# First small loads on ScalarE's queue, new hand-written lists for the beginning and the end, and the FFN middle of the last two tiles in three column parts

## The reference: what is computed

```
states = scan(state @ A.T + x_t @ B.T)              # 16 states
out = layernorm(states @ C.T + x @ D.T) * gamma + beta
x = layernorm(x + out)
gate, up = fp4(x) @ fp4(w_gate).T, fp4(x) @ fp4(w_up).T    # 704 columns each
x = layernorm(x + fp4(silu(gate) * up) @ fp4(w_down).T)
```

## Time and profile before

| | |
|---|---|
| median of 3 runs | 566.85 us (566.63 to 566.96) |
| profiled execution, its own time | 566.68 us |
| its span (first to last instruction) | 564.9 us, so 1.8 us lie around it |
| busy share of the span | PE 98%, DVE 92%, ACT 83%, POOL 88% |
| granted clock of TensorE, mean | 0.998 |
| chain that ended last, by engine | PE 90%, DVE 5%, ACT 2% |

### The profile page before, as it was taken

How to read it: one execution, slowest core, us unless ns; L and a number is a source line. 1 busy time by engine, 2 the same in 40 slices (tenths; PEclk the granted TensorE clock), 3 DMA queues, 4 the chain that set the end, 5 groups by cost and what they waited for, 6 DMA issues and landing times.

```text
span 564.9 us, 12830 instructions
## 1 busy us (share of the span) xinstructions
PE 551.6 (98%) x3751; PEld 495.0 (88%) x3751; DVE 518.0 (92%) x1241; ACT 468.3 (83%) x1415; POOL 494.4 (88%) x674
## 2 busy tenths in 40 slices
PE   9899999999999999999999999999999999999995
PEld 7577779999999999999999999999999999999894
DVE  4896799999999999999999999999999999999973
ACT  3557867889888998988889898888989888898756
POOL 2566887999999999999999999999999999998653
PEclk9999999999999999999999999999999999999999
DMA  8951000011121111111211111121111122100001
GB/s 291 383 182 30 5 24 24 22 41 47 56 61 60 52 60 58 49 50 59 59 52 56 58 50 50 59 59 55 54 59 49 50 59 59 56 22 19 20 20 46
DMA packets 35772, 36.25 MB, mean 64 GB/s; under 512 B 6752, under 2 KB 34464, under 8 KB 34720
## 3 DMA queue, kind: packets, MB, share of 16 engines
q1 hardware_dynamic: 35744, 35.90, 20.1%
HBM read 19.50 MB, written 8.39 MB: 49 GB/s over the span
## 4 chain that ended last, share of the span: by engine, by line
PE 90%; DVE 5%; ACT 2%; issue 1%; POOL 0%; POOLq 0%; DVEq 0%; ACTq 0%
PE gu L1434 41%; PE turned L1434 18%; PE yb L1434 8%; PE turned L1517 7%; PE turned L1460 2%; PE yb L1448 1%; PE grid L1293 1%; PE turned L1541 1%; PE turned L1540 1%; PE gu L1345 1%; PE yb L1345 1%; DVE scratch L1095 1%; DVE scratch L1133 1%; PE gu L1381 1%; PE turned L1381 1%
## 5 line engine op out<-in xcount | busy, mean ns | idle before, releaser
L1434 PE MATMUL gu<-wguHi,xtHi 128*128 128x512 f32 (+1 forms) x384 | 151.3, 394 | 0.4 <-DVE xtLo L1088 0.4
L1434 PE MATMUL gu<-wguLo,xtHi 128*128 128x512 f32 (+1 forms) x384 | 143.7, 374 | 0.0
L1434 PE MATMUL gu<-wguHi,xtLo 128*128 128x512 f32 (+1 forms) x384 | 143.7, 374 | 0.0
L560 POOL TENSOR_TENSOR scratch<-scratch 128x704 f32<-128x704 f32 x63 | 90.7, 1439 | 3.2 <-DVE scratch L1109 2.6
L571 POOL TENSOR_TENSOR scratch<-scratch 128x640 f32<-128x640 f32 x64 | 81.4, 1271 | 7.6 <-DVE scratch L1133 7.4
L1434 PE MATMUL turned<-wdHi,htHi 128*128 128x256 f32 x295 | 83.7, 284 | 0.0
L1434 PE MATMUL turned<-wdHi,htLo 128*128 128x256 f32 x295 | 83.6, 283 | 0.0
L1434 PEld LDWEIGHTS gu<-wguHi,xtLo 128*128 128x128 f32 x384 | 72.2, 188 | 12.3
L1434 PE MATMUL turned<-wdLo,htHi 128*128 128x256 f32 x295 | 82.6, 280 | 0.0
L1434 PEld LDWEIGHTS gu<-wguHi,xtHi 128*128 128x128 f32 x384 | 72.2, 188 | 9.9 <-DVE xtLo L1088 1.1
L1434 PEld LDWEIGHTS gu<-wguLo,xtHi 128*128 128x128 f32 x384 | 72.4, 189 | 8.2
(11 more groups left out here) (225 smaller groups left out, 1679.7 us busy)
## 6 DMA issues: line engine op xcount, KB each, us to landing
xT<-in_L_attn_x_dram SPq DMA_DIRECT2D x8, 1024.0 KB, 9.9
scratch<-in_L_attn_x_dram SPq DMA_DIRECT2D x64, 128.0 KB, 2.4
out_dram<-scratch SPq DMA_DIRECT2D x64, 128.0 KB, 1.9
xtTile<-xT SPq DMA_DIRECT2D x48, 128.0 KB, 2.1
stTile<-statesHi SPq DMA_DIRECT2D x128, 8.0 KB, 1.7
stTile<-statesLo SPq DMA_DIRECT2D x64, 8.0 KB, 1.7
scratch<-in_L_ffn_w_down_dram SPq DMA_DIRECT2D x1, 704.0 KB, 10.3
scratch<-in_L_ffn_w_up_dram SPq DMA_DIRECT2D x1, 640.0 KB, 8.9
```

What stands on the lines that cost most here:

```text
L560: nc.gpsimd.tensor_tensor(blocks(hx[:, m % 2, :]), blocks(hx[:, m % 2, :]), each_block(hRc[:, m % 4, :], FB), ALU.mult).then_inc(s_xnh, 1)
L1434: ins = nc.tensor.matmul(to, l, r, start=(first and q == 0), stop=(last and q == len(passes) - 1))
```

## The change

Four things are changed. (1) The loads of D, C, A and B are issued by ACT and no longer by SP, and SP issues the last two weight loads ahead of the `tMat` copies. (2) All lists of the beginning are in another order, with 8 instead of 12 `unread` first, and `d_prep` and `w_recip` have their independent steps interleaved. (3) The last two tiles (`SPLIT = 2`) run their FFN middle in three parts of 256, 256 and 192 columns, products of gate and up included. (4) The end is written out as lists, without the `unread` of `is_ending` (one is left ahead of each of the last two `down`), and the last two tiles are normalised by one DVE operation (`norm_last`) instead of `nr3` and `norm3`.

```diff
-    VECTOR_COPIES = (0, 2, 7, 9, 14, 15, 17, 19, 23, 25, 28)
+    VECTOR_COPIES = (2, 3, 5, 9, 12, 15, 16, 17, 18, 19, 27, 28)
...
-            for i in range(last):
+            for i in range(last if eng is nc.sync else 0):
                 step(HALVES, i, False)
...
-        SPLIT = 1
+        SPLIT = 2
+        FIRST_SPLIT = TILES - SPLIT
+        PARTS = ((0, 2 * P), (2 * P, 4 * P), (4 * P, FF))
...
@@ SP @@
-                sp.dma_start(dRaw[:, :, :], D.rearrange("(k p) d -> p k d", p=P)).then_inc(s_dc, 16)
-                sp.dma_start(cRaw[:, :, :], C.rearrange("(k p) n -> p k n", p=P)).then_inc(s_dc, 16)
-                sp.dma_start(aRaw[:, :], A).then_inc(s_small, 16)
-                sp.dma_start(bRaw[:, :], B).then_inc(s_small, 16)
             load_x(0)
...
+            sp.dma_start(wg[:, full + 1:WG_ROWS, :],
+                         w_up[P - part:FF, :].rearrange("(r p) k -> p r k", p=P)).then_inc(s_wload[2], 16)
+            sp.dma_start(wX[:, WG_ROWS * H:].rearrange("p (r k) -> p r k", k=FF),
+                         w_down.rearrange("(r p) k -> p r k", p=P)).then_inc(s_wload[3], 16)
             sp.wait_ge(s_tDiag, 1)
             sp.wait_ge(s_pwc, POWER_COPIES[LOG_C + 1])
...
@@ ACT @@
+                nc.scalar.dma_start(dRaw[:, :, :], D.rearrange("(k p) d -> p k d", p=P)).then_inc(s_dc, 16)
+                nc.scalar.dma_start(cRaw[:, :, :], C.rearrange("(k p) n -> p k n", p=P)).then_inc(s_dc, 16)
+                nc.scalar.dma_start(aRaw[:, :], A).then_inc(s_small, 16)
+                nc.scalar.dma_start(bRaw[:, :], B).then_inc(s_small, 16)
...
@@ DVE @@
+            def norm_last(h, m):
+                r = m % RING
+                dve.wait_ge(s_st[r], done_dma(h, m - RING))
+                dve.wait_ge(s_pow3, done(h, m))
+                nc.vector.tensor_scalar(outTile[:, r, :], x1[:, m, :], nm3t[:, m:m + 1], rs3[:, m:m + 1], ALU.add,
+                                        ALU.mult).then_inc(s_out, 1)
...
@@ PE @@
-                if is_ending(h, m):
-                    unread(4, to)
...
+            def down_part(h, m, k):
+                tile, to = h * CHUNK + m, down_bank(h, m)
+                if k == 0:
+                    pe.wait_ge(s_x1p, TILES)
+                    pe.wait_ge(s_r, tile)
+                    unread(1, to)
+                pe.wait_ge(s_lo, part(tile, k))
...
-            unread(12, wbanks[1], ones)
+            unread(8, wbanks[1], ones)
```

More of the change, by code:

```diff
@@ new lines, in _ @@
+            ve3(7, 0)
+            nr3(6, 7)
+            ve1(7, 7)
+            norm3(6, 7)
+            norm2(7, 6)
+            silu_gate(7, 3)
+            nm3(7, 1)
+            nr3(7, 0)
+            sq3(7, 1)
+            norm3(7, 0)
+            h_hi(7, 2)
+            nm2(7, 7)
+            h_abs(7, 3)
+            silu_gate(7, 4)
+            sq2(7, 7)
+            x_abs(7, 6)
+            ve2(7, 7)
+            x_hi(7, 5)
+            ve3(7, 1)
+            nr2(7, 7)
+            norm2(7, 7)
@@ new lines, in _ @@
+            nr3(7, 1)
+            norm3(7, 1)
+            nm3(7, 2)
+            sq3(7, 2)
+            ve3(7, 2)
+            h_hi(7, 3)
+            h_abs(7, 4)
+            silu_gate(7, 5)
+            x_abs(7, 7)
+            nr3(7, 2)
+            norm3(7, 2)
+            x_hi(7, 6)
+            nm3(7, 3)
+            sq3(7, 3)
+            silu_part(7, 6, 0)
+            ve3(7, 3)
+            h_hi(7, 4)
+            h_abs(7, 5)
+            silu_part(7, 6, 1)
+            nr3(7, 3)
+            norm3(7, 3)
@@ L1542, in ffn_down, with up_part, columns @@
                                  stop=True).then_inc(s_dn, 1)
+            def up_part(h, m, k):
+                tile, (a, b) = h * CHUNK + m, PARTS[k]
+                if k == 0:
+                    pe.wait_ge(s_xlo, done(h, m))
+                if is_split(tile - 1):
+                    pe.wait_ge(s_h, part(tile - 1, k))
+                else:
+                    pe.wait_ge([s_silu, s_h, s_hsc][k], tile)
+                def columns(w, c):
+                    return w[:, c, :].rearrange("p (g f) -> p g f", g=2)[:, :, a:b]
+                split_products(gu_part(k), [((xtHi[:, m % 2, c, :], xtLo[:, m % 2, c, :]),
+                                             (columns(wguHi, c), columns(wguLo, c))) for c in range(KH)]).then_inc(s_gate, 1)
@@ new lines, in turn_part @@
+            def turn_part(h, m, k):
+                tile = h * CHUNK + m
+                if k == 2:
+                    pe.wait_ge(s_lo, part(tile, 0))
+                elif is_split(tile - 1):
+                    pe.wait_ge(s_lo, part(tile - 1, 2 if k == 0 else 1))
+                else:
+                    pe.wait_ge(s_lo, tile)
+                pe.wait_ge(s_xlo, TILES)
+                pe.wait_ge(s_qh, part(tile, k))
+                for q in range(2):
+                    row = KD[2 * k + q]
+                    rows = hq[:, m % 2, row:row + P] if row + P <= FF else hTail[:, m % 2, :]
+                    ins = nc.tensor.transpose(ht_parts[k][:, q * P:(q + 1) * P], rows, ident[:, :])
+                ins.then_inc(s_t, 1)
```

748 lines of the change are left out of this document (482 added, 266 removed).

## The result

The changed kernel takes **584.82 us** (median of 5, 584.21 to 585.64) where the kernel before took 566.85 beside it: a ratio of 1.0316, interval 1.0296 to 1.0335. That is 18 us slower, where 1.5 us faster was forecast, and far outside the range. Both halves of the sum were wrong, the beginning most.

What follows compares the result with a forecast made beforehand. TensorE, busy 98% of the span, was taken to bound the kernel, its steady part unchanged. Beginning +2.9 and end −3.9 − 0.5 = −4.4 gave −1.5 us, 565.3 against the median of 566.85; range 560.8 to 568.2.

Steps and rivals of the forecast that it cites:

- The small loads now share the engines with x, so I let them land where they did.: Beginning, ACT's queue: D, C, A and B land when they did before, while x goes out 2.0 us sooner.
- Fillers, −1.8: Start of the kernel: eight filler matmuls instead of twelve unread's worth make TensorE ready 1.8 us earlier.
- I keep 2.4 GHz in the sum.: TensorE's clock, both halves: stays at full rate although fillers go, since the end's waits are short and split by products.
- Rival 2: Wait ahead of link(0, 8): the clock falls there, half rate loses another 2.7 us, whole +1.9, 568.7 us; chance 0.20.
- the third rival: End: DVE's extra operations bind the last two tiles, half of the gain is left, about 567.5 us; chance 0.10.
- The new wait on SP: Beginning: w_abs(0) ahead of powers(3) delays tMat and x 4 and 5 (19.4 instead of 15.24); beta_b lands at 36.6.
- Landing + 6.3 for `link(0, 8)`: Beginning: four add_beta, w_norm(3), w_abs(3), w_sum(3) and links follow beta_b's landing; link(0, 8) at 42.9, 0.9 us later.
- Behind `link(0, 8)`: +2.7: From link(0, 8) to gu0(0, 0): extra copies and pair_sums(2) ahead of layer(0, 0); gu0(0, 0) at 66.6, 3.6 later in all.
- The end: Behind the steady part: 3.9 us gained up to the last add_x1 and 0.5 by the last norm, together −4.4.
- fillers, parts and the last norm: End: fillers of 3.56 us go and 0.44 return, waits of three parts are 1.15 and 0.9, the norm saves 0.5.
- the last norm: End, behind the last add_x1: one DVE operation of 0.42 us in place of nr3 and norm3 saves 0.5 us.
- The range: Whole kernel: 560.8 to 568.2 us, said to leave out one in five.

Runs made afterwards that it cites:

- powers_first: Changed kernel with powers(1) to powers(3) directly behind powers(0) on PE and ACT, ahead of x transposes and w_abs(0): 581.71 us, ratio 1.0278.
- x_early: The kernel with the four mended places, and x transposes 20 to 23 moved back among the links with their copies: ratio 1.0085 against the kernel before.
- old_silu: Beginning of the kernel before, end of the changed kernel with silu_gate(7,3) moved up on ACT: 564.43 us, ratio 0.9957.
- mended end: The changed kernel's end with silu_gate(7,3) moved up on ACT; with the old beginning it takes 564.43 us, ratio 0.9957.
- the four mended places: Changed kernel with small loads on SP, powers first, first four add_beta behind w_norm(5), silu_gate(7,3) up: 573.98 us, ratio 1.0120.
- mended beginnings: Beginnings of the kernel with the four mended places (1.0120), of x_early (1.0085), and of x_early with add_beta between w_norm(3) and w_norm(4) (1.0100).

## Why the prediction was wrong, point by point

- **"The small loads now share the engines with x, so I let them land where they did."** This step failed first and worst. They are issued at the same times as before and land 3.4 to 4.8 us later (D 6.0 us from its issue instead of 2.6). The sentence beside it had the reason in hand: the engines are full, and a second queue adds nothing. I drew from it that x gains nothing, and not that D loses. Alone it costs 10 us.
- **Fillers, −1.8.** TensorE was ready earlier, but not its data: the eight end at about 4.8 us, and it then waits 3.18 for C and starts on D at 8.02, where it was 6.30 before. With the loads back on SP it starts at 4.39 or 4.64, and the gain is there.
- **"I keep 2.4 GHz in the sum."** Wrong. Rival 2 had the half rate, but gave it 2.7 us of loss and a chance of 0.20, and its cause was not the one that the trace shows. Its sign, a low clock in a window of 42 to 52 us, came true; but the clock had fallen by about 38.9, before the landing, with TensorE busy 2.00 of 2.00 us in every window from 34 on. What made it fall there is open. Behind the wait for C (3.18 us) and behind the hole at the end it fell with a wait ahead of it; the falls at 22 and at 76 us are not explained. With the loads alone moved it costs 6.4 us. (The working says that the half rate would give the sum of the third rival; it is the second.)
- **The new wait on SP.** The chain was right (`w_abs(0)`, `powers(3)`, `tMat`, x 4 and 5, `beta_b`), and so was its sign. The sizes were off: `tMat` at 20.16 for 15.5, x 4 at 23.96 for 19.4, the landing at 41.3 for 36.6. The term that was mis-sized is the start of `w_norm(0)`: 17.47 for the 13.1 that I took. It waits for `w_recip(0)`, which stands in DVE's list behind `d_prep` and three x copies. With the loads back on SP it starts at 14.58 and `tMat` goes out at 17.26, so about 3 us are the late D, and 1.5 remain with the copies ahead of it. I had also not followed PE's list, whose ten x transposes make the product of `powers(3)` nearly as late. And the DMA engines, which I had run dry for a microsecond, stand nearly idle from 20 to 24 us (share 0.04).
- **Landing + 6.3 for `link(0, 8)`.** It was landing + 7.6. `w_sum(3)` took 1.91 where I took 0.8; the last part, for which the working has 1.8 and the sum about 1, took 1.15. `w_sum(3)` was long beside `w_norm(4)` of POOL, with which it started (DVE, then POOL); in `powers_first`, where the same two start together at 44.33, it took 0.69 and `w_norm(4)` 1.94.

```profile
45.88 1.91 DVE L1167 SCALAR_TENSOR_TENSOR scratch<-scratch 128x512 f32<-128x512 f32 x1
```

```profile
45.86 1.38 POOL L498 TENSOR_TENSOR scratch<-scratch,wAm 128x704 f32<-128x704 f32 x1 [0.68 <-DVE wAm L1161]
```

- **Behind `link(0, 8)`: +2.7.** It was +8.6. I priced the operations that were moved, not that the moved ones used to stand in waits between the links and now stand on the path, part of them at half rate. Of the 8.6, 5.7 are TensorE's longer busy time and 2.9 its waits. `x_early` showed 2.2 us of it.
- **The end.** The terms for fillers, parts and the last norm were near: 39.8 us to the last `add_x1` in `old_silu` where I had 38.7, the last norm 0.6 for 0.5. The whole gain of the mended end is 2.7 us of 4.4, the difference being the 0.65 ahead of `layer(7, 7)` and products and waits behind it that take 1.1 longer. What failed is that I read ACT's list only in the beginning: the misplaced `silu_gate(7, 3)` turned the gain into a loss of 1.7 (55.98 to 57.68).
- **The range.** It was built from terms that could each be off by a microsecond or two, and several steps failed in the same direction. They also hold each other in part: the move of the loads costs 10 us alone in the old lists and gives back 3 in the new ones, where the landing and the clock hold the same links. But it is not all overlap: the four mended places gave 10.8 us together where their single gains add to 11.7.

What stays open: 7 to 11 us of the mended beginnings (`layer(0, 7)` at 98.12 to 102.12 where it was 91.25). The old lists as a whole give them back, as the run with the old beginning shows, and for the stretch behind `link(0, 8)` the rows name the waits and the clock that make them up; no single edit did, and what makes the clock fall among the links is not known.

## What to carry to other kernels

- A small load that the first work waits for belongs ahead of the large ones on their queue, or the large ones must be held back. On a second queue it is served beside them, and here that was 4 us of latency, then 10 us of kernel in one pair of lists and 3 in another.
- Price a wait on TensorE twice: for its length, and for the work behind it at half rate. Fillers that look like waste (98% busy) may be what keeps the rate, and the busy share does not show it: read the clock in windows. A long wait is not the only place where it falls.
- With lists written by hand, walk each engine's list against the one before for every operation that another engine waits for. One call eleven places too late cost 4.4 us, and moving one back without its partner on another engine cost again.
